# Selective scan on VectorE in two half-row steps, with the next product issued between them

## What is computed

```python
x = x + 0.5 * ffn(layernorm(x))
x = x + mixer(layernorm(x))
x = x + 0.5 * ffn(layernorm(x))
```

```python
dA  = exp(delta[..., None] * A[None, None])
dBu = delta[..., None] * Bm[:, :, None, :] * u[..., None]
def step(h, inp):
    dA_t, dBu_t, c_t = inp
    h = dA_t * h + dBu_t
    y = einsum('bdn,bn->bd', h, c_t)
    return (h, y)
```

## Time and profile before

| | us |
|---|---|
| median of 3 runs (lowest, highest) | 3139.1 (3138.5, 3139.45) |
| profiled execution, its own time | 3137.2 |
| its span, first to last instruction | 3135.4 |
| VectorE busy | 2657.3 (85%) |
| TensorE busy | 2657.7 (85%) |
| first to last scan start | 698.0 to 2569.9 |

### The profile page before, as it was taken

One profiled execution on the slowest core, in us unless ns is written; L12 is line 12 of the kernel. 1 busy time (PEld: TensorE's weight loads), 2 busy tenths in 40 slices (PEclk: granted clock), 3 DMA queues, 4 the chain that ended last, 5 costly groups with the idle time before them and its releaser, 6 DMA issues. The chain is left out here.

```text
span 3135.4 us, 31534 instructions
## 1 busy us (share of the span) xinstructions
PE 2657.7 (85%) x10285; PEld 1379.8 (44%) x10285; DVE 2657.3 (85%) x2498; ACT 1692.0 (54%) x2302; POOL 2149.1 (69%) x1283
## 2 busy tenths in 40 slices
PE   2999999967878978978978978978877669999998
PEld 1566657633314414414414414414412215666665
DVE  6788875549999999999999999999999996777775
ACT  3444444446665665666666666656665534444442
POOL 4566664348877877777777777777878864655553
PEclk9999999988978979979978979968976769999999
DMA  3011111037786786786786686776686760101100
GB/s 108 21 47 45 51 57 34 21 90 189 170 198 163 181 196 162 175 200 162 177 198 162 175 200 161 174 190 170 166 198 167 170 165 27 31 31 34 33 28 20
DMA packets 173144, 387.95 MB, mean 124 GB/s; under 512 B 22470, under 2 KB 89990, under 8 KB 172742
## 3 DMA queue, kind: packets, MB, share of 16 engines
q1 hardware_dynamic: 155302, 367.12, 47.1%
q10 hardware_dynamic: 17696, 19.01, 2.0%
HBM read 308.33 MB, written 52.56 MB: 115 GB/s over the span
## 5 line engine op out<-in xcount | busy, mean ns | idle before, releaser
L1320 POOL TENSOR_TENSOR mix_scan<-mix_scan,mix_bc 128x1024 f32<-128x1024 f32 x512 | 1205.2, 2357 | 394.7 <-DVE mix_scan L1404 394.1
L1404 DVE TENSOR_TENSOR_SCAN mix_scan<-mix_decay,ps_all 128x1024 f32<-128x1024 f32 x512 | 1170.2, 2285 | 62.1 <-ACT mix_decay L1360 19.4
L1459 PE MATMUL ps_all<-mix_stack,mix_sel 96*128 96x512 bf16 x1024 | 367.8, 447 | 366.1 <-DVE mix_scan L1404 352.8
L776 PE MATMUL ps_all<-ffn_w_gate_up,ffn_xT 128*128 128x512 f32 (+1 forms) x1536 | 650.6, 560 | 12.2 <-DVE ffn_h L514 9.9
L1415 DVE TENSOR_TENSOR ps_all<-ps_all,mix_bc 128x1024 f32<-128x1024 f32 x512 | 618.3, 1208 | 38.8 <-PE ps_all L1459 38.1
L1360 ACT ACTIVATE mix_decay<-mix_decay,mix_a_neg 128x1024 f32<-128x1024 f32 x512 | 573.7, 1141 | 118.9 <-DMA mix_decay<-delta_rows 117.9
L776 PEld LDWEIGHTS ps_all<-ffn_w_gate_up,ffn_xT 128*128 128x128 f32 x1536 | 277.5, 191 | 242.6 <-issue 198.2
L1459 PEld LDWEIGHTS ps_all<-mix_stack,mix_sel 96*128 96x128 bf16 x1024 | 78.8, 103 | 672.5 <-DVE mix_scan L1404 551.3
L514 DVE TENSOR_TENSOR ffn_h<-ffn_silu_gate,ps_all 128x704 f32<-128x704 f32 x128 | 113.6, 888 | 274.5 <-ACT ffn_silu_gate L697 271.0
L1441 PE MATMUL ps_all<-mix_scan,mix_red 128*32 128x512 f32 x2048 | 339.8, 745 | 4.8 <-POOL mix_scan L1320 4.8
L654 POOL TENSOR_TENSOR ffn_h_scaled<-ffn_h,ffn_h_recip 128x1408 f32<-128x1408 f32 x64 | 168.6, 2635 | 243.4 <-ACT ffn_h_recip L746 243.4
(11 more groups left out here) (137 smaller groups left out, 3692.4 us busy)
## 6 DMA issues: line engine op xcount, KB each, us to landing
mix_decay<-delta_rows SPq DMA_DIRECT2D x512, 512.0 KB, 7.3
mix_stack<-mix_parts SPq DMA_DIRECT2D x384, 64.0 KB, 2.0
delta_rows<-mix_delta SPq DMA_DIRECT2D x32, 512.0 KB, 3.1
ffn_x<-_attn_hidden_states_dram SPq DMA_DIRECT2D x32, 256.0 KB, 3.1
after_ffn<-ffn_y SPq DMA_DIRECT2D x32, 256.0 KB, 3.1
normed_ffn<-ffn_y_normed SPq DMA_DIRECT2D x32, 256.0 KB, 3.2
mix_x_tokens<-normed_ffn SPq DMA_DIRECT2D x32, 256.0 KB, 12.4
mix_x_residual<-after_ffn ACTq DMA_DIRECT2D x32, 256.0 KB, 4.1
```

What stands on the lines that cost most here:

```text
L776: ins = M(psG[:, lo:hi], xT[:, j % 2, (t * KX + k) * P:(t * KX + k + 1) * P], wgu[:, k, lo:hi], start=(k == 0), stop=(k == KX - 1))
L1320: G.tensor_tensor(wt, wt, bc[r % 2][:, 1, :], ALU.mult).then_inc(hc_done, 1)
L1404: V.tensor_tensor_scan(w[:, slot % RING, :], da[:, slot % SPREADS, :], ps_du[:, slot % 2, :], 0.0, ALU.mult, ALU.add).then_inc(scan_done, 1)
L1459: ins = M(ps_du[:, slot % 2, h * 512:(h + 1) * 512], const.sel[0:SEL, i, :], stack[:, c % 2, q, h * 512:(h + 1) * 512], start=True, stop=True)
```

## The change

Product and scan are cut into two halves of 512 columns. The first half's scan starts from 0, as before; the second starts from column 511 of the first half's result, which it reads from `w` as a [128, 1] operand, and it waits for the first one's `scan_done`. VectorE's order in a slot becomes: product of this slot's second half, scan of its first half, product of the *next* slot's first half, scan of its second half. `rep_du`, `dbu_done` and `scan_done` now count halves. TensorE's `replicate` works on one half each: the first half for slot + 1 stands ahead of `sum_quad`, the second behind it, each waiting for the scan of the same half two slots earlier. At the end of a round `replicate` and product go on into the next round. GpSimd and SyncE wait for the same scans as before, in the new count.

```diff
-                    sy.wait_ge(scan_done, n - SPREADS + (1 if s == SLOTS - 1 else 0))
+                    sy.wait_ge(scan_done, 2 * (n - SPREADS + (1 if s == SLOTS - 1 else 0)))
...
-                        pool.wait_ge(scan_done, R * 64 + (slot + 1))
+                        pool.wait_ge(scan_done, 2 * (R * 64 + slot + 1))
...
-            def scan(r, R, slot):
-                n = R * 64 + (slot + 1)
-                dve.wait_ge(exp_done, n)
-                dve.wait_ge(dbu_done, n)
-                if slot >= 8 or r > 0:
-                    dve.wait_ge(y_made, R * 16 + (slot - 8) // 4 + 1)
-                V.tensor_tensor_scan(w[:, slot % RING, :], da[:, slot % SPREADS, :], ps_du[:, slot % 2, :], 0.0,
+            def times_b(R, slot, h):
+                half = slice(h * 512, (h + 1) * 512)
+                dve.wait_ge(rep_du, 2 * (R * 64 + slot) + h + 1)
+                if slot == 0 and h == 0:
+                    dve.wait_ge(taken["B"], (R + 1) * 4)
+                V.tensor_tensor(ps_du[:, slot % 2, half], ps_du[:, slot % 2, half], bc[R % 2][:, 0, half], ALU.mult)\
+                 .then_inc(dbu_done, 1)
+
+            def scan(r, R, slot, h):
+                half = slice(h * 512, (h + 1) * 512)
+                to = w[:, slot % RING, half]
+                n = 2 * (R * 64 + slot) + h
+                dve.wait_ge(dbu_done, n + 1)
+                if h == 0:
+                    dve.wait_ge(exp_done, R * 64 + slot + 1)
+                    if slot >= 8 or r > 0:
+                        dve.wait_ge(y_made, R * 16 + (slot - 8) // 4 + 1)
+                    start = 0.0
+                else:
+                    dve.wait_ge(scan_done, n)
+                    start = w[:, slot % RING, 511:512]
+                V.tensor_tensor_scan(to, da[:, slot % SPREADS, half], ps_du[:, slot % 2, half], start,
                                      ALU.mult, ALU.add).then_inc(scan_done, 1)
...
-                    if core(r, full):
-                        n = R * 64 + (slot + 1)
-                        dve.wait_ge(rep_du, n)
-                        if slot == 0:
-                            dve.wait_ge(taken["B"], (R + 1) * 4)
-                        V.tensor_tensor(ps_du[:, slot % 2, :], ps_du[:, slot % 2, :], bc[r % 2][:, 0, :], ALU.mult)\
-                         .then_inc(dbu_done, 1)
-
-                    if s == GATE and (c > 0 or r >= 1) and core(r, full):
+                    if not core(r, full):
+                        continue
+                    if slot == 0 and r == 0:
+                        times_b(R, 0, 0)
+                    times_b(R, slot, 1)
+                    if s == GATE and (c > 0 or r >= 1):
                         gate(*((R, c - 1) if c > 0 else (R - 1, 3)))
-                    if core(r, full):
-                        scan(r, R, slot)
+                    scan(r, R, slot, 0)
+                    if slot < 63:
+                        times_b(R, slot + 1, 0)
+                    elif r < B - 1:
+                        times_b(R + 1, 0, 0)
+                    scan(r, R, slot, 1)
...
                 if slot > 1 or r > 0:
-                    pe.wait_ge(scan_done, R * 64 + (slot - 1))
-                for h in range(2):
-                    ins = M(ps_du[:, slot % 2, h * 512:(h + 1) * 512], const.sel[0:SEL, i, :],
-                            stack[:, c % 2, q, h * 512:(h + 1) * 512], start=True, stop=True)
-                ins.then_inc(rep_du, 1)
+                    pe.wait_ge(scan_done, 2 * (R * 64 + slot - 2) + h + 1)
+                M(ps_du[:, slot % 2, h * 512:(h + 1) * 512], const.sel[0:SEL, i, :],
+                  stack[:, c % 2, q, h * 512:(h + 1) * 512], start=True, stop=True).then_inc(rep_du, 1)
```

More of the change, by code:

```diff
@@ L1448, in sum_quad, with replicate @@
                     ins.then_inc(y_made, 1)
-            def replicate(r, R, slot):
+            def replicate(r, R, slot, h):
                 c, s = divmod(slot, SLOTS)
                 i, q = divmod(s, 4)
-                if s == 0:
+                if s == 0 and h == 0:
                     pe.wait_ge(stacked[c % 2], 16 * 12 * (R * 2 + (c // 2 + 1)))
                 if slot > 1 or r > 0:
-                    pe.wait_ge(scan_done, R * 64 + (slot - 1))
-                for h in range(2):
-                    ins = M(ps_du[:, slot % 2, h * 512:(h + 1) * 512], const.sel[0:SEL, i, :],
-                            stack[:, c % 2, q, h * 512:(h + 1) * 512], start=True, stop=True)
-                ins.then_inc(rep_du, 1)
+                    pe.wait_ge(scan_done, 2 * (R * 64 + slot - 2) + h + 1)
+                M(ps_du[:, slot % 2, h * 512:(h + 1) * 512], const.sel[0:SEL, i, :],
+                  stack[:, c % 2, q, h * 512:(h + 1) * 512], start=True, stop=True).then_inc(rep_du, 1)
             def program(r, R, full):
@@ L1466, in program @@
                     c, s = divmod(slot, SLOTS)
-                    if slot == 0 and core(r, full):
-                        replicate(r, R, 0)
-                    if slot < 63 and core(r, full):
-                        replicate(r, R, slot + 1)
+                    if r == 0 and slot == 0:
+                        for h in range(2):
+                            replicate(r, R, 0, h)
+                    if core(r, full):
+                        after_this = (r, R, slot + 1) if slot < 63 else (r + 1, R + 1, 0)
+                        if after_this[0] < B:
+                            replicate(*after_this, 0)
                     for h in range(2):
@@ L1476, in program @@
                             sum_quad(r - 1, R - 1, 15, h)
+                    if core(r, full) and after_this[0] < B:
+                        replicate(*after_this, 1)
                     for sl, kind, rel, n, bank, prev in jobs:
```

## The result

The changed kernel takes 3163.7 us (median of 16 runs, 3142.4 to 3165.6) against 3139.1 (16 runs beside them, 3136.8 to 3141.5): 1.0066 times, interval 1.0052 to 1.0079. It is 0.66% slower; 3116 was predicted, in a range of 3106 to 3162. Its runs are wider spread than those of before: three lie between 3142 and 3149 with a mean granted clock of TensorE of 0.895 to 0.897, the other 13 between 3160 and 3166 with 0.883 to 0.889. The profiled execution is one of the 13, with a time of 3164.45 us, 27.2 above that of before.

A forecast was written before the change was run, and what follows sets the result against it. VectorE was taken to set the mixer's pace. Slots -22.5, gates -4.5 and lone jobs +3 made -24 us from the profiled 3137.2, then 1.9 for the runs' median: 3115, stated as 3116, range 3106 to 3162.

The forecast's parts named there:

- What bounds the kernel, and what the wait is worth: In the mixer, VectorE sets the pace; the product-to-scan dependence costs 0.175 us in each ordinary slot and would be covered.
- Added starts, f = 0.06: Two more VectorE starts a slot, each a fixed 0.06 us; with the removed wait, -22.5 us over the mixer.
- The start value, p = 0: Reading the second scan's start from SBUF: likeliest free, bounds 0 to 0.09 us a scan, 0 to +46 us.
- TensorE, "its slack is the same" and +3 us: Each half of replicate keeps its slack in the new order; lone jobs in slow stretches add 3 us.
- Late gates gone: Gates in the mixer no longer wait for TensorE, as sum_quad is done about 1.7 us earlier: -4.5 us.
- ScalarE's late exponentials stay: VectorE's scans keep waiting for ScalarE's late exponentials, 17 us, since the change does not order them.
- The start value is dear: Rival: the SBUF start operand costs what it costs ScalarE, 0.077 to 0.09 us; 3145 to 3163 us, chance 0.35.
- The third rival: TensorE takes the gain: tightened slots fall late, two more 1 us stops a round, 14 us: 3130; shared chance 0.17.

The follow-up runs named there:

- e1: Changed kernel with the constant 0 as start value of every scan, all waits kept: 3124.1 us, ratio 0.9943 to the kernel before.
- h1: Kernel before with TensorE's new order alone, sum_quad between the halves of replicate, VectorE and waits on whole slots: 3181.0 us, ratio 1.0126.
- h4: Changed kernel with the u * D matmuls of every fourth sum_quad moved behind the second half of replicate, nothing left out: 3140.8 us, ratio 0.9999.
- i2: Changed kernel with two jobs moved, a D job from slot 14 to 13 and a B job from slot 50 to 52: 3141.1 us, ratio 1.0003.
- e2: Changed kernel with both halves of replicate ahead of sum_quad, each half keeping its own wait: 3180.9 us, ratio 1.0119.
- h2: Changed kernel with light TensorE jobs (one matmul per sum in jobs P, C, Z, O; no u * D matmuls): 3058.9 us, ratio 0.9737.
- h3: Kernel before with light TensorE jobs (one matmul per sum in jobs P, C, Z, O; no u * D matmuls): 3069.5 us, ratio 0.9767.
- f3: Changed kernel run again unaltered: 3151.9, 3163.8, 3163.8 and 3163.6 us at clocks 0.890, 0.883, 0.883, 0.883.
- f1: Changed kernel without the two u * D matmuls that close every fourth sum_quad: 3140.7 us, ratio 1.0002.
- g1: Kernel before, whole slots, with the product written to SBUF, the scan in place there, and the next slot's product ahead of the scan: 3801.6 us, ratio 1.2108.

## Why the prediction was wrong, step by step

- *What bounds the kernel, and what the wait is worth*: right. VectorE sets the pace between stops, and the dependence is gone wherever TensorE is on time.
- *Added starts, f = 0.06*: right in kind, a little too high. Half product 0.585 and half scan 1.125 against 1.125 and 2.20 for the whole ones give 0.045 and 0.05; two plain pairs make 3.42 instead of 3.445, which is 13 us in the change's favour. The measured 3.48 is that plus the operand.
- *The start value, p = 0*: this step failed, inside its bounds. The operand costs 0.062 us, 32 us in all, and by that and the smaller f VectorE's own part is -5 instead of -22.5. It is nearer to f than to ScalarE's 0.09. e1 shows it to be enough to turn the sign: without it the changed kernel is even with the kernel before or faster, with all its stops for TensorE.
- *TensorE, "its slack is the same" and +3 us*: this step failed too, and by more: stops for replicate are +44 us, +50 with the lost overlap. It has two parts. The text compared each half with its own release and need, and looked at what stands ahead of a *second* half only once, for slot 14, with a sum_quad that starts on time and has no u * D matmuls. sum_quad was held to run "in time that TensorE spent waiting", but in the slots that count TensorE has no such time: it arrives late from the last slot's jobs, and sum_quad with its u * D matmuls then takes 3.7 us at the low clock. h1 shows the order alone to cost 41 us in the kernel before, h4 that a part of it costs 23 in the changed one. And the slack of 4.5 instead of 5.8 us, which the text had right, was priced at 3 us for lone jobs; i2 shows the bursts of slots 14 and 50 alone to be worth 23 (not to be added to h4's 23: in slot 51 it is the same lateness). e2 shows that the old order isn't the remedy either: with the halves' waits the pair ahead of sum_quad is 17 us slower still.
- *The two together.* The sum said -24 us, the ledger says +26.5. VectorE's part is 17.5 us of the difference, TensorE's and ScalarE's together are 33. Take the operand's 32 us out of the ledger and -5.5 is left; leave only the added stops' 50 us out and it is -23.5. So neither miss alone would have made the kernel slower, it took both.
- *Late gates gone*: right, 1.1 us is the last one's, outside the loop.
- *ScalarE's late exponentials stay*: wrong, they went (-17 us). That they hide under the waits for TensorE is not shown: h2 and h3 wait for TensorE alike, and h3 has 8.8 us of late exponentials, h2 none. The cause stays open.
- *The rivals.* "The start value is dear" spans 3145 to 3163, and the measured 3163.7 lies 0.7 us above it, 1.7 above the stated range. That it comes so close is luck: the operand cost 32 us, not 39 to 46, and the rest is TensorE's. The third rival was this case in kind, at 14 us instead of 44. The trace of before had the warning: TensorE busy for 85%, a product already 2.47 us late, and durations that double with the clock.

What stays open: whether the low clock in slots 49 to 51 follows from the new pattern of TensorE's pauses. f3 shows that clock and lateness go together in one program, not which comes first. Nor is it settled how the 44 us of added waits divide between the place of sum_quad and the shorter slack: a late second half makes the next first half late too, and h4 and i2 are worth 23 us each alone and 34 together. Both also ran at a higher clock than the changed kernel (0.890 to 0.895 and 0.887 to 0.891 against 0.883 to 0.889 in most of its runs); f1, at 0.869, shows that the gain doesn't need it.

## What to carry to other kernels

When work on one engine is cut into halves over a two-deep buffer, the feeding engine's slack falls from two whole pieces to one and a half (here 5.8 to 4.5 us of other work); list the longest runs of other work that can stand ahead of *each* piece, at the feeder's slow clock, before counting the start-up costs of the pieces. Work put between two halves because the feeder usually idles there is late exactly in the slots where it does not idle. A [128, 1] operand is not free on VectorE: here it cost 0.062 us a scan, three quarters of the 0.08 us that the new order gained in a slot.

## What the runs showed of the hardware

- A VectorE scan with its start value in SBUF lasts 1271 ns, with a constant 1209 (512 columns), and the distance from start to start grows by as much (1.185 against 1.125 us). With the constant in all 1024 scans and every wait kept (e1), all last 1209.
- A VectorE scan with both inputs in SBUF and a GpSimd product with both inputs in SBUF take turns, g1 above: the scan takes 2.28 us alone and 3.56 where it starts 1.41 us before the GpSimd product ends; the product takes 2.36 us, and 4.34 where it starts during the scan. The Trainium skill (SBUF — State Buffer, Who interferes with whom, and SBUF: two separate sides) calls the port pair that VectorE with two SBUF inputs and GpSimd share an exclusive lock, held for a whole instruction; the trace agrees.
- TensorE's matmuls take twice as long at the low level of the granted clock (B jobs 3.78 us against 1.98), and the same program fell into runs some 20 us apart, 3 of 16 at a mean clock of 0.895 to 0.897 and 13 at 0.883 to 0.889.
